# Third layer's attention: value products cut in two around the context products, the context's high part between the exponentials, value copies behind the shares

## What is computed

```python
def _cross_attention(q_in, kv_in, wq, bq, wk, bk, wv, bv, wo, bo, bias_k, bias_v):
    qh = (q_in @ wq + bq).reshape(b, q_len, H, K)
    kh = (kv_in @ wk + bk).reshape(b, t, H, K)
    vh = (kv_in @ wv + bv).reshape(b, t, H, K)
    kh = jnp.concatenate([kh, jnp.broadcast_to(bias_k, (b, 1, H, K))], axis=1)
    vh = jnp.concatenate([vh, jnp.broadcast_to(bias_v, (b, 1, H, K))], axis=1)
    logits = jnp.einsum('bqhk,bthk->bhqt', qh, kh) / scale
    weights = jax.nn.softmax(logits, axis=-1)
    ctx = jnp.einsum('bhqt,bthk->bqhk', weights, vh).reshape(b, q_len, H * K)
    return ctx @ wo + bo
```

## Time and profile before

| what | us |
|---|---|
| median of 3 runs | 2281.2 |
| lowest and highest of them | 2280.79, 2281.65 |
| span of the profiled execution | 2282.1 |
| PE busy in the span | 2157.6 (95%) |
| DVE busy | 1466.7 (64%) |
| ACT busy | 1278.9 (56%) |
| POOL busy | 652.8 (29%) |
| the 128 steps of the third layer's attention | about 717 to 1767 |

### The profile page before, as it was taken

How to read it: one execution, slowest core, us unless ns; L and a number is a source line. 1 busy time by engine, 2 the same in 40 slices (tenths; PEclk the granted TensorE clock), 3 DMA queues, 4 the chain that set the end, 5 groups by cost and what they waited for, 6 DMA issues and landing times. The chain is left out here.

```text
span 2282.1 us, 47742 instructions
## 1 busy us (share of the span) xinstructions
PE 2157.6 (95%) x18208; PEld 1791.4 (78%) x18208; DVE 1466.7 (64%) x2828; ACT 1278.9 (56%) x3300; POOL 652.8 (29%) x661
## 2 busy tenths in 40 slices
PE   6999979999896999999999999999998999999899
PEld 4666656888795888888888888888887886776678
DVE  5888844555444766666666666666666439999963
ACT  4777754565543444444445544444444548888863
POOL 4444311111126321020304212030101217677711
PEclk9999999999998999999999999999998899999999
DMA  4000020000102000010100000000001210000000
GB/s 134 16 16 11 2 57 1 2 2 2 38 1 79 24 31 17 17 31 10 38 1 24 24 24 24 10 29 1 1 1 38 74 40 19 2 2 2 2 10 29
DMA packets 33661, 50.58 MB, mean 22 GB/s; under 512 B 2592, under 2 KB 22048, under 8 KB 32416
## 3 DMA queue, kind: packets, MB, share of 16 engines
q1 hardware_dynamic: 33440, 47.53, 6.7%
HBM read 45.43 MB, written 2.10 MB: 21 GB/s over the span
## 5 line engine op out<-in xcount | busy, mean ns | idle before, releaser
L824 ACT ACTIVATE l_probs<-l_s_psum,l_neg_max 128x129 f32<-128x129 f32 x512 | 181.5, 368 | 266.7 <-DVE l_neg_max L887 266.7
L911 DVE TENSOR_TENSOR x<-x,l_o_psum 128x512 f32<-128x512 f32 x256 | 176.1, 688 | 189.6 <-PE l_o_psum L778 187.8
L809 ACT ACTIVATE l_KT<-l_k_psum,cols 128x512 f32<-128x512 f32 x128 | 88.3, 690 | 197.6 <-PE l_k_psum L114 197.6
L1443 DVE TENSOR_REDUCE l_neg_max<-l_psum 128x2 f32<-128x512 f32 x256 | 163.4, 683 | 47.9 <-PE l_psum L1233 47.4
L656 POOL TENSOR_TENSOR l_head_w_high<-l_head_raw,one 128x768 fp32r<-128x768 f32 x30 | 44.5, 1483 | 516.1 <-PE l_o_psum L778 516.1
L2495 POOL TENSOR_TENSOR l_probs<-l_probs,l_mask_add 128x512 f32<-128x512 f32 x128 | 161.9, 1287 | 76.9 <-DVE l_probs L2723 76.9
L778 PE MATMUL l_o_psum<-l_head_w_high,l_context_low 128*128 128x256 f32 x512 | 156.0, 305 | 8.6 <-DVE l_context_low L892 8.6
L892 DVE SCALAR_TENSOR_TENSOR l_context_low<-l_c_psum,cols,l_context_high 128x512 fp32r<-128x512 f32 x128 | 95.8, 749 | 105.3 <-ACT l_context_high L816 104.5
L1372 ACT ACTIVATE l_PT<-l_psum 128x512 f32<-128x512 f32 x256 | 132.2, 603 | 54.9 <-PE l_psum L1261 54.9
L2665 ACT ACTIVATE l_probs<-l_probs,l_neg_max 128x128 f32<-128x128 f32 x512 | 159.8, 396 | 5.5 <-DVE l_neg_max L2730 5.2
L778 PE MATMUL l_o_psum<-l_head_w_high,l_context_high 128*128 128x256 f32 x512 | 144.5, 282 | 3.4 <-DVE x L911 2.3
(11 more groups left out here) (320 smaller groups left out, 6339.1 us busy)
## 6 DMA issues: line engine op xcount, KB each, us to landing
l_head_raw<-in_l_heads SPq DMA_DIRECT2D x32, 384.0 KB, 3.0
l_w<-in_l_w SPq DMA_DIRECT2D x4, 1024.0 KB, 9.6
l_ctx_in<-in_ctx_T SPq DMA_DIRECT2D x16, 256.0 KB, 5.3
l_value_raw<-in_l_values SPq DMA_DIRECT2D x8, 512.0 KB, 3.6
l_value_rows<-in_l_rows SPq DMA_DIRECT2D x8, 512.0 KB, 5.0
l_x_in<-in_x_T SPq DMA_DIRECT2D x16, 128.0 KB, 2.2
l_x_in<-in_ctx_T SPq DMA_DIRECT2D x16, 128.0 KB, 2.7
values<-in_l_w SPq DMA_DIRECT2D x2, 1024.0 KB, 6.0
```

The source lines that it names most:

```text
L824: last = act.activation(probs[:, i, :], scores[:, i // 2, i % 2, :], ACT.Exp, bias=neg_max[:, i:i + 1], scale=1.0, accum_out=den[:, i:i + 1])
L911: dve.tensor_tensor(out=x, in0=x, in1=o_bank[:, :], op=ALU.add).then_inc(o_free, 1)
L1443: dve.tensor_reduce(neg_max[:, u % 2, qt, at:at + 2], bank[:, :].rearrange("p (e k) -> p e k", e=2), AX, ALU.max, negate=True).then_inc(fr ...
```

## The change

The value product of a period is cut at the half of its contraction: `value_a` (3 matmuls) stays in front of the context products, `value_b` (the other 3) goes behind them; both add into the same bank. The exponentials are cut in two: `probs_a` (batches 0 and 1) stands before the context's high part, `probs_b` (batches 2 and 3, with the signal `exp_done`) behind it. The copy of the values (`values_kept`, DVE) moves from the end of the period to behind the shares of the next period, in front of the first add. No instruction is added or removed; the three initial value products keep their place.

```diff
+    def values(i):
+        return [("value_a", 0, i), ("value_b", 0, i), ("values_kept", 0, i)]
@@
         step("share", 1)
+        if 0 < p and p + 2 < STEPS2:
+            steps.append(("values_kept", (p + 2) // 4, (p + 2) % 4))
         step("out_a", 2)
@@
-        if 0 <= p + 3 < STEPS2:
-            steps.append(("value", (p + 3) // 4, (p + 3) % 4))
-        step("probs", 0)
+        if p + 3 < STEPS2:
+            steps.append(("value_a", (p + 3) // 4, (p + 3) % 4))
+        step("probs_a", 0)
         step("context", 1)
+        step("probs_b", 0)
+        if p + 3 < STEPS2:
+            steps.append(("value_b", (p + 3) // 4, (p + 3) % 4))
@@
-            def value(u, i):
+            def value_half(u, i, t):
                 b = u % 4 * 4 + i
-                n = value_at["value", u, i]
+                return product(pe, v_bank[:, :], [part[:, t, b, :] for part in ctx_in],
+                               [part[:, u // 4 % 2, t, :] for part in value_w], start=(t == 0), stop=(t == 1))
+
+            def value_a(u, i):
+                n = value_at["value_b", u, i]
                 value_weights_wait(pe, u // 4)
                 if n:
                     pe.wait_ge(v_free, n)
-                for t in range(2):
-                    last = product(pe, v_bank[:, :], [part[:, t, b, :] for part in ctx_in],
-                                   [part[:, u // 4 % 2, t, :] for part in value_w], start=(t == 0), stop=(t == 1))
-                last.then_inc(v_full, 1)
+                value_half(u, i, 0)
+
+            def value_b(u, i):
+                value_half(u, i, 1).then_inc(v_full, 1)
@@
-            def exponents(s):
+            def exponents(which):
+                for i in which:
+                    last = act.activation(probs[:, i, :], scores[:, i // 2, i % 2, :], ACT.Exp,
+                                          bias=neg_max[:, i:i + 1], scale=1.0, accum_out=den[:, i:i + 1])
+                return last
+
+            def probs_a(s):
                 act.wait_ge(max_done, s + 1)
                 if s:
                     act.wait_ge(t_full, turn_at["turn", s - 1] + 1)
-                for i in range(4):
-                    last = act.activation(probs[:, i, :], scores[:, i // 2, i % 2, :], ACT.Exp,
-                                          bias=neg_max[:, i:i + 1], scale=1.0, accum_out=den[:, i:i + 1])
-                last.then_inc(exp_done, 1)
+                exponents(range(0, 2))
+
+            def probs_b(s):
+                exponents(range(2, 4)).then_inc(exp_done, 1)
```

More of the change, by code:

```diff
@@ L539, in attention2 @@
         out_at = order.place("out_a", "out_b")
-        value_at = order.place("value")
+        value_at = order.place("value_b")
         set_up = sem("set_up")
@@ L628, in value_weights @@
                 if 2 <= n + 1 < 8:
-                    sync.wait_ge(v_free, value_at["value", 4 * (n - 1) + 3, 3] + 1)
+                    sync.wait_ge(v_free, value_at["value_b", 4 * (n - 1) + 3, 3] + 1)
                     load_rows(n + 1)
@@ L759, in values_summed @@
                 pe.wait_ge(t_free, turn_at["turn", s] + 1)
-                pe.wait_ge(v_free, value_at["value", u, 3] + 1)
+                pe.wait_ge(v_free, value_at["value_b", u, 3] + 1)
                 if s:
@@ L789, in normed @@
                 last.then_inc(t_full, 1)
-            order.run({"query": query, "key": key, "value": value, "score": score, "turn": turn,
+            order.run({"query": query, "key": key, "value_a": value_a, "value_b": value_b, "score": score, "turn": turn,
                        "context": values_summed, "out_a": lambda s: out(s, 0), "out_b": lambda s: out(s, 1),
@@ L849, in value_weights @@
                     act.activation(high, value_raw[:, :], ACT.Copy).then_inc(first_value_high, 1)
-            order.run({"query": query, "key": key, "context": context_high, "probs": exponents,
+            order.run({"query": query, "key": key, "context": context_high, "probs_a": probs_a, "probs_b": probs_b,
                        "normed": normed, "heads": heads, "value_weights": value_weights})
@@ L894, in context_low, with values_kept @@
                     .then_inc(c_free, 1)
-            def value(u, i):
-                dve.wait_ge(v_full, value_at["value", u, i] + 1)
+            def values_kept(u, i):
+                dve.wait_ge(v_full, value_at["value_b", u, i] + 1)
                 if u == 0 and i == 0:
```

8 lines of the change are left out of this document (4 added, 4 removed).

## The result

The changed kernel takes 2254.5 us (median of 4 runs, 2252.3 to 2256.3) where the kernel before took 2281.4 beside it: a ratio of 0.9877, 95% interval 0.9863 to 0.9891. The forecast was 2251, in a range of 2246 to 2266. The profiled execution spans 2254.1 us, 28.0 less than before.

A forecast was written before the change was run, and what follows sets the result against it. PE, fully busy inside the attention's 128 steps, was taken as the bound. Terms of -21.3, -7.3, -1.7, -1.2, +1.6 and -0.5 sum to -30.4 us, taking 2281.2 to 2250.8; predicted 2251, range 2246 to 2266.

The forecast's parts named there:

- Ordinary steps: First output half of 97 steps: the 0.22 us lost waiting for the context's low part goes, -21.3 us.
- Both inputs of the high part come at the same moment: Ordinary step: ACT free and context products ended together, near 1574.02; moving only one would gain nothing.
- Steps with statistics: 8 steps where DVE runs value copy, statistics, low part: statistics start 1.3 us earlier, -7.3 us.
- Held scalings: Two steps where DVE's scaling is held beside a POOL subtraction: part of the overlap goes, -1.7 us together.
- Transposes: Layer norm transposes now behind value_b: a third fp32-to-512-column place, 18 halves at 0.09, +1.6 us.
- The copy's and the exponentials' landing: DVE from share to first add, ahead of the second output half: 0, slack 0.02 to 0.14 us.
- rival (a): First add becomes late, holding the second output half: 0.11 to 0.23 us per step, 2263 to 2275; chance 0.19.
- One share that POOL holds: Share at 771.47 lasting 2.93 us beside a POOL subtraction: -0.5 us, between +0.6 and -1.6.
- The last steps: Steps without value products, losing 0.65 us twice: high part 0.5 earlier, -1.2 us, bounds 0 and -2.
- the only DVE instruction to fear: DVE's multiplication of the shares, moved by 0.6 us; the moved value copy, one input in PSUM, never blocks.
- (b): Slower: a late context holds ACT with two exponentials behind it; 0.5 us late makes +10 us, 2291; chance 0.04.
- (c): No change: the low part's wait passes to another PE input, such as the key copy; 2277 to 2285; chance 0.03.

The follow-up runs named there:

- e5: Changed kernel with the value copy behind the first add instead of in front of it; 2250.8 us, ratio 0.9857 to the kernel before.
- e2: Changed kernel with the four exponentials in one piece again, keeping PE's order and the moved value copy; 2284.4 us, ratio 1.0012 to the kernel before.
- e4: Changed kernel with the value copy back behind the value products, PE's and ACT's parts kept; 2274.1 us, ratio 0.9971 to the kernel before.
- e11: Changed kernel with the copy behind the first add and POOL's head 21 weights held until the seventh scaling; 2249.9 us, ratio 0.9849 to before.
- e3: Changed kernel with only the value copy's move kept, PE's and ACT's order as before; 2301.4 us, ratio 1.0097 to the kernel before.
- e1: Changed kernel with only ACT's split exponentials kept, PE's order and the copy as before; 2277.3 us, ratio 0.9985 to the kernel before.
- e9: Changed kernel with the layer norm's transposes ahead of the second value half, directly behind the context; 2252.3 us, ratio 0.9863 to before.

## Why the prediction was right, point by point

**The mechanism and the sign were right, the sum was 1.5 us too large**: -30.4 against -28.3 between the first and the last query product and -0.5 just behind the last (see the last steps below). The time was 3.5 us above the forecast of 2251; the other 2.0 us are less than the parts ahead of and behind the steps vary by. That the sum came so near is partly luck. The ordinary steps, the held scalings and the five steps with value weights came out 4.4 us worse than the sum had them (with 0.1 from the steps with statistics), the transposes, the share at 771 us and the first steps 2.8 better.

*Ordinary steps, -21.3 for 97.* Measured: 0.20 each in 86 steps (-17.4), 0.21 in the 6 with a first transposed half (-1.3), and what the five collision steps would have gained by e5 (-1.0): -19.7. The stall itself went whole: averaged over the 86 steps, the first output half takes 0.71 instead of 0.92. The term was 0.02 per step too large because the stall was 0.21 and not 0.22, and because the key products between the output halves take 0.01 more. The split costs nothing: the values take 0.09 more in two pieces, the queries behind them 0.09 less.

*"Both inputs of the high part come at the same moment."* Wrong, though harmless here. By e2 ACT is free 0.34, not 0.50, behind the start of the last exponential; the context alone released the high part. The high part's new start, 0.85 behind the first exponential, came out as I had it (0.86), for another reason: ACT is free 0.70 behind it (0.36 for the second exponential's start, and 0.34), and the context's end, 1551.03 + 1.05, is what releases it. I had that end at 0.82, and it is at 0.81.

*Steps with statistics, -7.3.* -7.2, to 7.82 like the others. e4 shows that this term is the copy's, and that the copy behind an earlier context but ahead of the statistics would have made them worse by 0.9 each.

*Held scalings, -0.7 and -1.0.* The step at 1292 us gave -1.0. The one at 1257 us gave nothing: the failed step is that I moved the overlap without placing it. Before, that scaling took 3.67:

```profile
1255.34 3.67 DVE L874 SCALAR_TENSOR_TENSOR l_xn<-x,l_mean_var,l_rstd 128x256 f32<-128x256 f32 x4
...
1254.50 1.47 POOL L656 TENSOR_TENSOR l_head_w_high<-l_head_raw,one 128x768 fp32r<-128x768 f32 x1
```

It started 0.84 behind POOL's multiplication; in the changed kernel it starts 0.34 behind it and lasts 4.19, 0.5 longer, and most of what the moved copy gives is gone. The copy in front of the add takes the rest: with it behind the add (e5) the step comes to 10.08. e11 shows what the collision is worth, 1.9 us.

*Transposes, +1.6.* Wrong: about zero. I counted the changes from fp32 to the 512-column products and found a third. I did not count that transposes that stand directly behind the context start late in the kernel before, a cost of 0.08 that goes. By kind, the second halves' steps show 0.0, the steps behind them +0.09, and the first halves' -0.09 beyond the stall.

*The copy's and the exponentials' landing, 0.* Right, and with more in hand than I had said: 0.24 instead of 0.02 to 0.14. I took 0.71 from share to copy where it is 0.61, and kept the load 0.12 to 0.23 ahead of its matmul where the rows of e2 and e3 show 0.03. Against that, I had taken the add's signal at the low part's 0.06, where it takes 0.12. With the count of the prediction, rival (a) had too high a chance.

*One share that POOL holds, -0.5.* It gave -1.5, near the end of its range. DVE and POOL at 771 us in the changed kernel:

```profile
770.87 1.22 DVE L935 TENSOR_TENSOR l_probs<-l_probs,l_rden 128x512 f32<-128x512 f32 x1
...
770.23 1.31 POOL L679 TENSOR_TENSOR l_value_rows<-l_value_rows 128x512 f32<-128x512 f32 x1
771.49 2.86 POOL L685 TENSOR_TENSOR l_value_w_low<-l_value_raw,l_value_w_high 128x1024 fp32r<-128x1024 f32 x1
```

Before, the share started at 771.47, 0.03 us behind the start of the long POOL subtraction, and lasted 2.93. Here it comes between two POOL instructions: DVE waits for the short one (1.22 in all), and the long one waits for DVE (2.86 instead of 2.40). Less than a tenth decides which engine stands: in e2 the share starts 0.01 behind the subtraction and lasts 2.95; in e4 it starts 0.09 ahead of it and lasts 0.69, and the subtraction takes 2.86. In e1 the share keeps its place in the step but POOL's instructions come 0.66 later, so that it starts 0.61 ahead of the subtraction; that is most of e1's gain.

*The last steps, -1.2.* Right. One of the two gave -0.7 (7.43 to 6.72). The other lies behind the last query product, outside the distance: from that product to the first key product behind it 3.29 before and 2.76 in the changed kernel, -0.5.

*Not in the sum: the five value-weight steps, +1.9.* This is the term that was missing. The prediction said that the moved multiplication of the shares was the only DVE instruction to fear, and then looked at one place, the one where the trace of before already showed a collision. The places where the trace of before shows a near miss were not looked up, and five of them became hits when the share moved 0.64 us forward against POOL's row.

**The rivals.** (a) occurred in the five steps and behind the two held scalings (10.29 to 10.08 and 8.37 to 8.19 in e5), not in the ordinary ones of the changed kernel, and at 0.37 us each for an add 0.64 late, where the price foreseen was 0.11 to 0.23 for each step. (b) did not. ACT does idle 0.15 ahead of the high part (1551.97 to 1552.12), over the 0.1 that I had named as its sign; but this sign was set with the wrong 0.50, and what (b) needs, a high part later than 0.86 behind the first exponential, is not there. (c) is ruled out by the waits. What stays open is the 1.5 us in the part ahead of the first step, which varies between runs by more than that, and what PE's part would do by itself.

## What to carry to other kernels

When a late operand is the end of a chain over three engines, moving one link can show nothing or a loss: here ACT's part is worth -1.7 us, PE's with the copy -0.9, the copy +20, PE's with ACT's -5.9, and all three -28. So judge such a change by the slack of each link, not by its parts. When an instruction that needs a resource shared with another engine is moved, go through every instruction of that engine around the new place, the near misses of the old one above all. And count what a place costs on both of its sides: the saving of 0.1 behind the transposes was paid back ahead of them. And look at each stall, not only at the total: in e2 the first stall had mostly gone, and a new one behind it hid that.

## What the runs showed of the hardware

- The start of an ACT activation of 512 columns can follow 0.34 us behind the start of an exponential of 129 columns with its accumulator (1500.60 to 1500.94 in e2).
- A weight load that was held starts 0.12 us behind the end of the DVE add that releases it, its matmul 0.03 later, and the matmul behind that 0.19 to 0.20 later where it would be 0.12 (e2 and e3). A matmul that is late by x there thus costs x + 0.07.
- Which of DVE and POOL stands when both need SBUF goes by the order of their starts, and less than a tenth of a us settles it: 2.95 us for a share that starts 0.01 after POOL's 2.40 us subtraction (e2), 0.69 for one that starts 0.09 before it, with 2.86 for the subtraction (e4).
- The one that stands is longer by the overlap of the two rows less about 0.15 us: 0.69, 0.84 and 1.33 us for overlaps of 0.14, 0.29 and 0.79 (before, e2, changed).
- Two places on PE cost 0.08 to 0.09 us each: transposes directly behind the context products start 0.89 behind their start, a value product 0.81 (e9, changed kernel), and a 512-column product behind fp32 matmuls is followed 0.32 later instead of 0.23.
